# Moving four pieces of work over the loop's jump in a transformer-Mamba kernel

## The reference

```
x = x + attention(q = layernorm(x), k = v = ctx, mask)        16 heads of 32, 257 keys, biases
x = x + mamba(layernorm(x))                                   d_inner 1024, 16 states, 4 taps
x = x + ffn(layernorm(x))                                     2048, activations and weights quantised
```

## Time and profile before

| | |
|---|---|
| profiled execution | 2040.91 us |
| its span | 2039.1 us, granted clock 0.975 |
| TensorE busy (matmul) | 1876.9 us, 92% |
| VectorE busy | 1825.7 us, 90% |
| ScalarE busy | 1623.5 us, 80% |
| GpSimd busy | 496.5 us, 24% |
| DMA | 190.74 MB, mean 94 GB/s |

### The profile page before, as it was taken

One profiled execution on the slowest core, in us unless ns is written; L12 is line 12 of the kernel. 1 busy time (PEld: TensorE's weight loads), 2 busy tenths in 40 slices (PEclk: granted clock), 3 DMA queues, 4 the chain that ended last, 5 costly groups with the idle time before them and its releaser, 6 DMA issues. The chain is left out here.

```text
span 2039.1 us, 43896 instructions
## 1 busy us (share of the span) xinstructions
PE 1876.9 (92%) x14989; PEld 1297.8 (64%) x15004; DVE 1825.7 (90%) x2193; ACT 1623.5 (80%) x4441; POOL 496.5 (24%) x392
## 2 busy tenths in 40 slices
PE   7898999999999999999899999999898989678799
PEld 5576666767676666666676667666666657366444
DVE  1546999999999999999999999999999999989788
ACT  3358888897978888888879897888888888867484
POOL 1001314131414132141413141413214131201013
PEclk9999999999999999999999999999999999788899
DMA  8623433332333333343333334343333333320214
GB/s 289 219 80 90 87 95 84 93 80 84 85 105 74 102 74 75 94 90 94 84 89 82 93 79 111 70 95 86 75 94 85 93 78 86 97 84 11 73 41 145
DMA packets 91485, 190.74 MB, mean 94 GB/s; under 512 B 16692, under 2 KB 37828, under 8 KB 86088
## 3 DMA queue, kind: packets, MB, share of 16 engines
q1 hardware_dynamic: 76376, 133.32, 20.5%
q0 software_dynamic: 14832, 54.01, 14.5%
HBM read 116.12 MB, written 17.18 MB: 65 GB/s over the span
## 5 line engine op out<-in xcount | busy, mean ns | idle before, releaser
L1481 ACT ACTIVATE dA<-dt,A_sb 128x124 f32<-128x124 f32 x2048 | 618.4, 400 | 5.1 <-DVE dt L1805 5.0
L1855 DVE TENSOR_TENSOR_SCAN hb<-dA,hb 128x2048 f32<-128x2048 f32 x118 | 522.4, 4427 | 10.2 <-ACT dA L1481 6.5
L1005 PE MATMUL bank<-ctxT,wk_sb 128*128 128x256 f32 x2048 | 469.9, 384 | 26.2 <-ACT Q L1358 15.7
L1016 PE MATMUL bank<-wv_sb,ctxT 128*128 128x512 f32 x1024 | 469.8, 599 | 2.3 <-ACT ctxT L1291 2.3
L1005 PEld LDWEIGHTS bank<-ctxT,wk_sb 128*128 128x128 f32 x2048 | 380.7, 191 | 96.3 <-ACT Q L1358 21.4
L1016 PEld LDWEIGHTS bank<-wv_sb,ctxT 128*128 128x128 f32 x1024 | 186.2, 191 | 190.4 <-issue 185.1
L1583 POOL DMA_DIRECT2D hb<-hb x103 | 93.3, 906 | 833.6 <-DVE hb L1861 818.1
L1850 DVE TENSOR_TENSOR hb<-u,BC 128x2048 f32<-128x2048 f32 x118 | 270.5, 2292 | 5.7 <-DVE u L1817 2.6
L1861 DVE TENSOR_TENSOR hb<-hb,BC 128x2048 f32<-128x2048 f32 x117 | 269.4, 2303 | 1.5
L1114 PE MATMUL bank<-xn2T,win_sb 128*128 128x128 f32 x2048 | 243.6, 282 | 0.7 <-ACT xn2T L1387 0.7
L1114 PEld LDWEIGHTS bank<-xn2T,win_sb 128*128 128x128 f32 x2048 | 241.9, 198 | 3.4 <-issue 1.3
(11 more groups left out here) (169 smaller groups left out, 2474.4 us busy)
## 6 DMA issues: line engine op xcount, KB each, us to landing
hb<-hb POOLq DMA_DIRECT2D x103, 512.0 KB, 5.2
ctx_sb<-in_ctx_dram SPq DMA_DIRECT2D x64, 512.0 KB, 3.9
BC<-bcd_dram SPq DMA_DIRECT2D x32, 1024.0 KB, 7.0
maskb<-in_mask_Bx1x1xS_fk_dram SPq DMA_DIRECT2D x64, 128.5 KB, 3.5
wstage<-in_L_ffn_w_dram SPq DMA_DIRECT2D x4, 2048.0 KB, 11.4
x_sb<-in_x_dram SPq DMA_DIRECT2D x16, 256.0 KB, 4.0
win_sb<-in_L_attn_in_proj_w_dram SPq DMA_DIRECT2D x1, 4096.0 KB
bo_sb<-bias_dram SPq DMA_DIRECT2D x64, 64.0 KB, 2.2
```

Source lines behind the costliest of these rows:

```text
L1005: last = pe.matmul(bank[6 + j][:, (m % 2) * KF:(m % 2 + 1) * KF], wk_sb[:, c, m * P:(m + 1) * P], ctxT[:, c, :], start=(c == 0), stop=(c = ...
L1016: last = pe.matmul(bank[h][:], ctxT[:, c, h * P:(h + 1) * P], wv_sb[:, c, :], start=(c == 0), stop=(c == DC - 1))
L1481: last = act.activation(dA[:, c % 2, n * BT:(n + 1) * BT, 1:], dt[:, c, :].rearrange("p (b s) -> p b s", s=S)[:, :, 1:], ACT.Exp, scale=A_ ...
L1855: ins = dve.tensor_tensor_scan(flat, dA[:, c % 2].rearrange("p n s -> p (n s)"), flat, 0.0, ALU.mult, ALU.add)
```

## The change

```diff
-        FINISH = {(0, "a"): range(21, 22), ...
+        FINISH = {(0, "x"): range(20, 21), (0, "a"): range(21, 22), ...
-                 (3, "e"): range(19, 21)}
+                 (3, "e"): range(19, 20)}
@@ def tail(part):
+            part.wo_product(LAST, 0)
             part.weights_transpose(range(0, 8))
             part.x1_write(LAST)
             part.mamba_norm(LAST)
+            part.scans(PREV, range(20, 21))
@@ def interval(ta, tm, to, more):
                     if b == 0 and front:
+                        part.wo_product(tm, DC * (g + 1))
                         part.x1_write(tm)
+                        part.mamba_norm(tm)
+                    if b == 0:
+                        place("x")
                     if b == 0 and here:
                         part.load_bias(ta)
                         part.residual(ta)
@@
                     if here:
                         part.scores(g, ta, b, to)
-                    if b == 0 and front:
-                        part.mamba_norm(tm)
@@
                     if here:
                         part.softmax(g)
+                    if b == 0 and front:
+                        part.mamba_rows(tm)
                     if b == 0:
                         place("a")
+                    if b == 3 and here and more:
+                        part.q_product(ta + 1)
+                        part.q_spread(ta + 1)
                     place("m")
                     if b == 1 and front:
                         part.rows_load(tm, 0)
                     if b == 2 and here and more:
                         part.ln_q_rows(ta + 1)
-                    if b == 3 and here and more:
-                        part.q_product(ta + 1)
-                        part.q_spread(ta + 1)
@@
                     if b > 0:
                         place("n")
-                    if b == 0 and front:
-                        part.mamba_rows(tm)
@@ end of the interval
-                    if b == 3 and here:
-                        part.wo_product(ta, keys)
```

More of the change, by code:

```diff
@@ L332, in perceiver_kernel @@
         DONE = {step: k + 1 for k, step in enumerate(CHAIN)}
-        FINISH = {(0, "a"): range(21, 22), (0, "b"): range(22, 26), (0, "c"): range(26, 28),
+        FINISH = {(0, "x"): range(20, 21), (0, "a"): range(21, 22), (0, "b"): range(22, 26), (0, "c"): range(26, 28),
                   (1, "a"): range(28, 29), (1, "t"): range(29, 31), (1, "p"): range(31, 32)}
```

## The result

The changed kernel takes 2069.78 us (median of 4 runs, 2068.29 to 2071.03); the kernel before, run beside it, takes 2040.27. The ratio is 1.0146 (95% interval 1.0129 to 1.0164): slower by 29.5 us, where +19 was forecast. All lines of the file behind the schedule move by two: x1 is L1767 (was L1765), the scan L1857 (L1855), the score passes L1740 (L1738), the reciprocal L1753 (L1751).

The account below looks back on a forecast made before the run. An interval was taken to last VectorE's work plus TensorE's stretch from Wx to Wout. Jump +13.8, hole +14.3 and taps -9 gave +19 us, 2060 us; the forecast's own range was 2050 to 2068, the outer 2040 to 2072.

Parts of the forecast that it names:

- the fallen clock: Rival: the new 1.5 us stall at Wx lowers TensorE's clock in the stretch closing the interval; +10, 2070 us, chance 0.13.
- Which engine closes the interval: Claim: VectorE's work plus TensorE's stretch from Wx to Wout sets the interval; TensorE's norm-row stalls lie outside.
- Parts 1 and 2 (Wo, Q): Product with Wo behind the jump; Q's product and copies ahead of four decays; each priced 0.
- Part 3, the jump: VectorE's scan moved behind the jump, leaving the shorter multiply ahead of it: +1.25 a jump, +13.8 us for 11.
- Gap 2.15 in place of 0.90: VectorE's idle time per jump: 1.85 ahead of x1 plus 0.3 at the scan, against 0.90 before.
- The second stop: VectorE's sequencer stands again 2.5 us behind the restart; expected just ahead of the scan or under it, taken as 0.3.
- Part 3, the hole: Statistics no longer fill VectorE's wait for exponentials at the reciprocal: +1.02 in each of 14 intervals, +14.3 us.
- Part 4, taps: Norm rows sooner, VectorE at its taps 2 us later: the 0.86 wait goes in 7 intervals, -9 us.
- gap stays: Rival: VectorE's gap at the jump stays as it is; +5, 2046 us, chance 0.17.
- jump costs nothing: Rival: VectorE's jump is hidden behind the multiply; -5, 2036 us, chance 0.10.
- TensorE sets the end: Rival: the interval closes through the norm rows, so VectorE drops its waits for TensorE; -28, 2013 us, chance 0.10.
- The clock falls inside the loop: Rival: the stall at Wx slows TensorE's closing stretch, 1.4 us lost each second interval; +10 on top, 2070 us, chance 0.13.

## Why the prediction was right in kind and short in size

The direction and the mechanism came as forecast: a jump laid bare, a hole at the reciprocal, the taps' wait gone. The size did not: 2069.8 lies above the forecast's own range, which ended at 2068, and the outer range reached it only for the fallen clock. Of the signs named beforehand, the intervals last 113.2 us on average (112.5 forecast), and TensorE's wait for the norm rows is 1.5 on average but up to 2.7 (below 2 forecast).

- **Which engine closes the interval:** right. TensorE's waits for norm rows and Q fell by 30 us and nothing was gained, as it waits as much elsewhere; VectorE's wait for Wout kept its 11.3 us.
- **Parts 1 and 2 (Wo, Q), 0 each:** right, by a run each. TensorE's jump is bare, as allowed for (2.2 us, not 1), and x1 does not see it as long as VectorE's own fetch is 4.4 us.
- **Part 3, the jump, +13.8:** this is the term that was mis-sized, "Gap 2.15 in place of 0.90". It measured 3.2 (2.4 ahead of x1, 0.8 ahead of the scan), +25.4 us over the loop, and lies above the bound of +2 a jump. Both halves were too small. The restart was taken at 3.4 to 3.9 us from two jumps, with the DMA named as a guess for the longer one. The guess is now shown, but it should have been carried on: issued some 2.3 us earlier, the branch stands 1.75 us behind the DMA at ten jumps of 11 (4.07 in the kernel before), and the fetch takes 4.4. The second stop was taken to be covered by the scan, but for 0.3. The sequencer's records say why it is not: the scan's own register instructions come at 1024.35 and 1024.46, behind the semaphore wait of the statistics at 1024.21, and the scan follows at 1025.32 only. With the scan alone behind the jump no such wait is between x1 and it; there the scan starts at 1027.00 and the sequencer's records stop from 1026.94 to 1028.51, under it. And 0.41 of the 0.8 needs no jump at all, which the forecast did not have.
- **Part 3, the hole, +1.02 an interval:** right, 0.93 (11.2 us in twelve intervals), and filling it gave 9.4 back.
- **Part 4, taps, -9:** right, -8.1, and without regard to the clock, as forecast; the wait for SiLU at Wx is 11.9 us in 9 times, 1.3 each, against some 1.5 forecast.
- **The rivals:** "gap stays", "jump costs nothing" and "TensorE sets the end" are out. "The clock falls inside the loop" gave the right total (2070) by the wrong way: behind Wx the clock is at 1.00 in the changed kernel. That its number is the measured one is luck. It came true only when the jump's cost was taken out.

## What to carry to other kernels

On the engine that closes the loop, put a long instruction last ahead of a loop's jump, and look for what DMA was started just before: the fetch ran beside it here. In these traces an instruction hid a stop of its sequencer only where it had been issued before the stop. When a step is moved off a gap that it filled, price the gap first; and once it is priced, ask whether fewer jumps isn't the simpler edit, as it was here.

## What the runs showed of the hardware

- The time from VectorE's branch to the first instruction of the next pass depends on when GpSimd has started a 512 KB accumulating DMA: 2.9 to 3.4 us where that was 4.07 us ahead of the branch (kernel before, ten jumps), 3.9 where it was 2.5, 4.38 to 4.49 where it was 1.75, and 2.87 where it was only 0.18. With 64 KB of it, 1.75 us before, it is 2.77 to 3.07.
- In the two kernels with the product with Wo ahead of the jump and the scan behind it, TensorE's branch is 2.8 us ahead of VectorE's (5.8 in the changed kernel) and most fetches last 4.8 to 5.0. The changed kernel with the product moved back shows that this goes with the product's place; whether the two fetches disturb each other is not shown.
- A VectorE multiply of 2048 columns lasts 3.0 in place of 2.29 us beside a GpSimd sum of 512 columns that is still running when it starts.
- A 1.8 us stall of TensorE at Wx was followed by a granted clock of 0.66 in ten intervals of one kernel and of 1.00 in another interval of it and in five of another kernel; what sets them apart is open.
